# A graph and expert network on one core: down projections loaded from two queues, the last router moved into the first step

## The reference

```python
logits = xf @ gate_w.T                              # 8 experts
topk_w, idx = jax.lax.top_k(logits, 2)
topk_w = jax.nn.softmax(topk_w, axis=-1)
h = jax.nn.silu(jnp.einsum('td,ehd->teh', xf, w1))  # w1: 8 x 1024 x 512
eo = jnp.einsum('teh,edh->ted', h, w2)              # w2: 8 x 512 x 1024
routed = jnp.einsum('te,ted->td', comb, eo)
shared = jax.nn.silu(xf @ sg_gate.T) * (xf @ sg_up.T) @ sg_down.T
x = x + routed + shared
```

## Time and profile before

| | busy us | share | instructions |
|---|---|---|---|
| PE | 589.2 | 95% | 3046 |
| PE's weight loads | 482.8 | 77% | 3046 |
| DVE | 500.8 | 80% | 592 |
| ACT | 430.3 | 69% | 529 |
| POOL | 105.9 | 17% | 112 |

### The profile page before, as it was taken

How to read it: one execution, slowest core, us unless ns; L and a number is a source line. 1 busy time by engine, 2 the same in 40 slices (tenths; PEclk the granted TensorE clock), 3 DMA queues, 4 the chain that set the end, 5 groups by cost and what they waited for, 6 DMA issues and landing times.

```text
span 623.3 us, 9254 instructions
## 1 busy us (share of the span) xinstructions
PE 589.2 (95%) x3046; PEld 482.8 (77%) x3046; DVE 500.8 (80%) x592; ACT 430.3 (69%) x529; POOL 105.9 (17%) x112
## 2 busy tenths in 40 slices
PE   4899999998899999999999999999979989999997
PEld 4677888876688876888888888887768778888886
DVE  6799989884689967898888989898776777777773
ACT  4787787844298859677878787876435766666673
POOL 3100000001000000000000000000011656666666
PEclk9999999999999999999999999999999989999999
DMA  7789999983659966989999999996289989999920
GB/s 252 252 299 307 387 386 385 337 300 107 201 185 343 323 231 235 350 329 341 328 342 355 328 357 331 338 324 221 83 188 215 261 213 266 262 262 262 231 54 17
DMA packets 102224, 168.11 MB, mean 270 GB/s; under 512 B 10683, under 2 KB 30140, under 8 KB 102182
## 3 DMA queue, kind: packets, MB, share of 16 engines
q1 hardware_dynamic: 99876, 165.72, 83.1%
q10 hardware_dynamic: 2322, 2.07, 1.2%
HBM read 167.51 MB, written 0.26 MB: 269 GB/s over the span
## 4 chain that ended last, share of the span: by engine, by line
PE 80%; DVE 11%; ACT 5%; issue 2%; POOL 1%; DMA 1%; SPq 0%; ACTq 0%; DVEq 0%
PE pre L839 31%; PE y L839 31%; PE wt L819 6%; PE tp L851 5%; DVE w_lo L1234 3%; PE pre L846 1%; ACT w_hi L551 1%; DVE w_lo L1221 1%; DVE st L1172 1%; DMA ends<-in_edge_weight 1%; PE y L936 1%; POOL rstd L476 1%; ACT w_hi L538 1%; PE wt L1063 1%; PE pre L952 0%
## 5 line engine op out<-in xcount | busy, mean ns | idle before, releaser
L1234 DVE TENSOR_TENSOR w_lo<-raw,w_hi 128x2048 fp32r<-128x2048 f32 x115 | 259.0, 2287 | 40.0 <-ACT w_hi L551 39.5
L551 ACT ACTIVATE w_hi<-raw 128x2048 fp32r<-128x2048 f32 x116 | 218.6, 1918 | 0.0
L839 PE MATMUL pre<-w_hi,x_hi 128*128 128x512 f32 x292 | 85.1, 404 | 4.0 <-ACT x_hi L556 3.3
L538 ACT ACTIVATE w_hi<-wt 128x512 fp32r<-128x512 f32 x88 | 52.2, 600 | 51.5 <-PE wt L819 50.9
L839 PE MATMUL pre<-w_lo,x_hi 128*128 128x512 f32 x292 | 83.3, 398 | 1.4 <-DVE w_lo L1234 0.9
L606 ACT ACTIVATE hT_hi<-tp 128x512 fp32r<-128x512 f32 x66 | 39.6, 600 | 65.1 <-PE tp L851 65.1
L1221 DVE TENSOR_TENSOR w_lo<-wt,w_hi 128x512 fp32r<-128x512 f32 x88 | 58.5, 668 | 31.2 <-ACT w_hi L538 31.0
L839 PE MATMUL pre<-w_hi,x_lo 128*128 128x512 f32 x292 | 82.9, 397 | 0.0
L839 PE MATMUL y<-w_hi,hT_hi 128*128 128x512 f32 x280 | 81.9, 414 | 0.0
L475 POOL TENSOR_SCALAR rstd<-mv 128x1 f32<-128x1 f32 x11 | 3.0, 272 | 441.1 <-DVE mv L1173 441.1
L839 PE MATMUL y<-w_lo,hT_hi 128*128 128x512 f32 x280 | 75.9, 392 | 0.4 <-DVE w_lo L1234 0.4
(11 more groups left out here) (266 smaller groups left out, 689.6 us busy)
## 6 DMA issues: line engine op xcount, KB each, us to landing
raw<-in_L_ffn_w SPq DMA_DIRECT2D x80, 1024.0 KB, 7.0
raw<-in_L_ffn_W SPq DMA_DIRECT2D x32, 1024.0 KB, 10.2
raw<-in_L_ffn_w SPq DMA_DIRECT2D x32, 512.0 KB, 11.2
raw<-in_L_gnn_Wr SPq DMA_DIRECT2D x8, 1024.0 KB, 6.2
raw<-in_L_gnn_Wl SPq DMA_DIRECT2D x8, 1024.0 KB, 6.6
raw<-in_L_gnn_W SPq DMA_DIRECT2D x2, 1024.0 KB, 7.1
raw<-in_L_ffn_sg_gate SPq DMA_DIRECT2D x2, 1024.0 KB, 8.1
raw<-in_L_ffn_sg_up SPq DMA_DIRECT2D x2, 1024.0 KB, 7.7
```

Of the source, the lines that this page charges most:

```text
L538: act.activation(w_hi[:, g % SPLIT_SLOTS, q], wt[q % 2][:], ACT.Copy).then_inc(w_hi_ready, 1)
L551: act.activation(w_hi[:, g % SPLIT_SLOTS], raw[:, g % RAW_SLOTS], ACT.Copy).then_inc(w_hi_ready, 4)
L839: last = pe.matmul(dst, xs[:, k], ws[:, k], start=start and i == 0, stop=stop and i == len(passes) - 1 and bias is None)
L1234: dve.tensor_tensor(w_lo[:, i], raw[:, g % RAW_SLOTS], w_hi[:, i].bitcast(F32), ALU.subtract).then_inc(w_lo_ready, 4)
```

## The change

1. The four DMAs of a down pair are shared: SP issues q = 0 and 1, at the places where it issued all four; ACT issues q = 2 and 3, with the same waits. ACT does this for pair 0 in the attention layer behind the copy of qT (L773), for pair 2 behind the ReLU for `fT` (L800), and for pair s+2 in the even steps s = 2 to 14 behind the quarters and ahead of SiLU.
2. The router's logits go between the two products of step 0 on PE. DVE reads them out and makes the maximum at the head of step 0, ACT's exponential stands behind the second quarter of step 0, and the rest of `route_l3` stands on DVE behind the quarters of step 1.
3. On ACT, SiLU of step 0 stands behind the quarters, as in all other steps.
4. BRIDGE for the last mixture is 6 instead of 14.

```diff
@@ -27,7 +27,7 @@
 RAW_SLOTS = 8
 SPLIT_SLOTS = 4
 
-BRIDGE = {"l0g": 0, "l0f": 4, "l1f": 37, "l2g": 23, "l2f": 30, "l3g": 28, "l3f": 14}
+BRIDGE = {"l0g": 0, "l0f": 4, "l1f": 37, "l2g": 23, "l2f": 30, "l3g": 28, "l3f": 6}
 SIM_AT = 12
 FIRST_HOTS = 2
 EARLY_COUNTS = 4
@@ -65,7 +65,7 @@
         self.turned = turned
         self.summed = summed
         self.act, self.lead = act, lead
-        self.route = lead or 1
+        self.route = 0 if lead else 1
         self.selected = selected
 
     def chunk(self, s):
@@ -309,6 +309,11 @@
             wv = w.rearrange("e (k c p) n -> e p k c n", c=KC, p=P)
             return wv[at(u // U, 4 // U, it)][:, u % U]
 
+        def pair_rows(slot, q):
+
+            rows = raw[32 * q:32 * q + 32, slot:slot + 2].rearrange("j s c n -> j (s c n)")
+            return rows.rearrange("j (b m) -> j b m", m=2 * P)
+
         def half_rows(w, u):
 
 
@@ -385,9 +390,8 @@
                     wait_split(sp, G_L3G + slot - 1)
                 else:
                     sp.wait_ge(w_blocked, at(4 * (v - 2), 4 * LOOP_BLOCKED, it))
-                for q in range(4):
-                    dst = raw[32 * q:32 * q + 32, slot:slot + 2].rearrange("j s c n -> j (s c n)")
-                    sp.dma_start(dst.rearrange("j (b m) -> j b m", m=2 * P), columns[q]).then_inc(landed[slot], 16)
+                for q in range(2):
+                    sp.dma_start(pair_rows(slot, q), columns[q]).then_inc(landed[slot], 16)
 
             def square(w):
                 return w.rearrange("(c p) n -> p c n", p=P)
@@ -549,6 +553,17 @@
                 else:
                     act.wait_ge(landed[g % RAW_SLOTS], at(arrived(g), 16, it))
                     act.activation(w_hi[:, g % SPLIT_SLOTS], raw[:, g % RAW_SLOTS], ACT.Copy).then_inc(w_hi_ready, 4)
+
+            def load_down(v, it=None):
+
+                slot = raw_slot(BLOCKED[v])
+                columns = both_halves(A["L3_ffn_sg_down"] if v == 0 else A["L3_ffn_w2"][at((v - 2) // 2, 2, it)])
+                if v < 4:
+                    wait_split(act, G_L3G + slot - 1)
+                else:
+                    act.wait_ge(w_blocked, at(4 * (v - 2), 4 * LOOP_BLOCKED, it))
+                for q in (2, 3):
+                    act.dma_start(pair_rows(slot, q), columns[q]).then_inc(landed[slot], 16)
 
             def round_x(tag, plain):
 
@@ -608,8 +623,6 @@
 
                 def shared_step(s, g, it=None):
 
-                    if s == 0:
-                        activate(s)
                     turning = G_L3F + 3 if s == 0 else turned_within(g) if s < pipe.n else None
                     if turning is not None:
                         act.wait_ge(chunk_done, at(turning - SPLIT_SLOTS + 1, 8, it))
@@ -619,15 +632,18 @@
                             round_turned_quarter(turning, q, it)
                         if 0 <= v < pipe.n and s < pipe.n:
                             round_block(BLOCKED[v], q, it)
-                    if 0 < s < pipe.n:
+                        if s == pipe.route and q == 1:
+                            after0()
+                    if s >= 2 and s % 2 == 0 and s + 2 < pipe.n:
+                        load_down(s + 2, it)
+                    if s < pipe.n:
                         activate(s, it)
                     if 1 <= s <= pipe.n:
                         high_turned(s, it)
                     if s == pipe.n - 2:
                         for q in range(4):
                             round_block(BLOCKED[s], q)
-                    if s == pipe.route:
-                        after0()
+
                 for s in range(4):
                     step(s)
                 with act.Fori(0, pipe.loops()) as it:
@@ -771,6 +787,8 @@
             act.activation(h[:, 1], pre[1][:], ACT.Copy).then_inc(sm("l3g_k"), 1)
             act.wait_ge(sm("l3g_qT"), 1)
             act.activation(scratch[:, 2 * D:3 * D], tp[:], ACT.Copy).then_inc(sm("l3g_qTs"), 1)
+            load_down(0)
+
             def turned_pair(g, first):
 
                 if first == 0:
@@ -798,6 +816,7 @@
             turned_pair(G_L3F + 1, 2)
             act.wait_ge(sm("l3g_f1"), 1)
             act.activation(fT[0:32, :], ms[0:32, 0:P], ACT.Relu, bias=l3b1[:, 0:1]).then_inc(sm("l3g_f1s"), 1)
+            load_down(2)
             turned_pair(G_L3F + 2, 0)
             turned_pair(G_L3F + 2, 2)
             round_x("l3f", True)
@@ -887,6 +906,8 @@
                         low = (sm("xlo"), nth("xlo", pipe.tag))
                     if s < pipe.lead:
                         product(g, pre[s % 2][:], x_hi, x_lo, True, True, low=low)
+                        if s == 0:
+                            router()
                         product(g + 1, y[s % 2][:], x_hi, x_lo, True, True)
                     elif s < pipe.n:
                         bias = None
@@ -896,7 +917,7 @@
                                     bias_hl[:, col:col + D])
                         product(g, pre[s % 2][:], x_hi, x_lo, True, True, it, bias, low)
                         g += 1
-                    if s == 0:
+                    if s == 0 and not pipe.lead:
                         router()
                     if s == 3 and seeded:
                         turn_gates(pipe.tag, E8)
@@ -1273,6 +1294,8 @@
                 def step(s, it=None):
                     g = pipe.chunk(s)
                     if pipe.lead:
+                        if s == pipe.route:
+                            router[0]()
                         turning = G_L3F + 3 if s == 0 else turned_within(g) if s < pipe.n else None
                         for q in range(4):
                             if turning is not None:
@@ -1282,8 +1305,8 @@
                     if s < pipe.n:
                         split_chunk(g + AHEAD, it)
                         g += 1
-                    if s == pipe.route == 2:
-                        router()
+                    if s == 1 and pipe.lead:
+                        router[1]()
                     if s == 3 and seeded:
                         copy_gates(pipe.tag)
                     if 1 <= s <= pipe.n:
@@ -1608,16 +1631,18 @@
             split_turned_quarter(G_L3F + 2, 3)
             low_x("l3f")
 
-            def route_l3():
+            def logits_l3():
                 logits_in("l3f", E8)
                 negative_max("l3f", E8)
+
+            def route_l3():
                 dve.wait_ge(sm("exp"), nth("exp", "l3f"))
                 link(top(row[:, 0, 0:E8], E8, 2, row[:, 1, 0:E8], row[:, 2, 0:E8]))
                 link(dve.reduce_sum(row[:, 7, 3:4], row[:, 2, 0:E8], AX_X))
                 link(dve.reciprocal(row[:, 7, 4:5], row[:, 7, 3:4]))
                 link(dve.memset(gates[:, 0:1], 1.0))
                 link(dve.tensor_scalar(gates[:, 1:1 + E8], row[:, 2, 0:E8], row[:, 7, 4:5], None, ALU.mult))
-            pipeline(L3F, route_l3, 1, False)
+            pipeline(L3F, (logits_l3, route_l3), 1, False)
 
 
 _INS = ["x", "src", "dst", "edge_weight", "L0_gnn_emb_1", "L0_gnn_emb_2", "L0_gnn_alpha_p", "L0_gnn_beta_p",
```

## The result

The changed kernel takes 643.97 us (median of 4 runs, 641.47 to 647.17) against 627.42 for the kernel before beside it: a ratio of 1.026 (95% interval 1.022 to 1.030). It is slower by 16.5 us where I had forecast 2.9 us faster. The profiled execution took 643.1 us with a span of 641.4, 18.1 longer than the span before.

A forecast was written before the change was run, and what follows sets the result against it. TensorE, busy 95% of the span near full clock, was taken as the bound. Router -2.77, bridge -0.25 and ScalarE's issues +0.1 gave -2.9 us, taking the 627.52 median to 624.6; range 622.7 to 628.4.

The forecast's parts named there:

- the steady steps: Last dense layer, ten steps of 7.71 us, PE busy throughout at full clock: reordering could win nothing, only lose.
- The router: Moved to steps 0 and 1 of the last layer: losses 1.85 instead of 4.62 us, gain 2.77.
- Step 3: Last layer: its 3.98 us loss, from a 2.14 us wait of PE and lower clock, would go.
- the wait for the later SiLU: PE's third turn of step 1, last layer: wait near 1.0 us, 1.15 lost with a restart; bounds 0.5 to 2.4.
- that in step 2: PE's wait in step 2, last layer: near 0.4 us; step loss 0.7, upper bound 1.5; router taken as 2.2.
- B: Rival, step 0: SiLU's table load waits until ACT is empty, 1.28 us more; 627.6 us in all; chance 0.07.
- E: Rival, step 0: the exponential still takes its own table load, 1.28 us more; 625.5 us in all; chance 0.05.
- The bridge: Ahead of the last layer, BRIDGE 14 to 6: -0.25 us; bounds -0.25 to +1.7 if the clock stays low.
- ScalarE's issues: Half of each down pair issued by ACT, nine pairs: +0.1 us, 0 in steady steps; SyncE's gain worth nothing.
- Rival C: Steady steps: ACT's halves land late, each of seven pairs holds PE 1.0 to 1.1 us; 632 us; chance 0.10.
- The limit: Steady steps: ACT's pieces may take 12.5 us from issue to landing before PE is held.
- The landing: Down-pair pieces land after 7.5, 11.4, 15.6 us (least, median, most); ACT's would be behind none of SyncE's.

The follow-up runs named there:

- e2: Kernel before with the change's router and SiLU places alone, all loads on SyncE, BRIDGE 14: 624.74 us, ratio 0.9961.
- e7: Kernel before with BRIDGE 6 instead of 14 and nothing else: 627.89 us, ratio 1.0024.
- e8: As e2, with 18 filling transposes in PE's wait ahead of the last turned quarter before the layer, and BRIDGE 16: 623.50 us, ratio 0.9955.
- e5: As e1, but ScalarE issues its later pieces at the end of the step before, right behind hT_hi: 626.20 us, ratio 0.9995.
- e12: As e1, but each later up chunk loads only half its rows, 512 KB: 627.56 us, ratio 1.0002.
- e3: The whole change with BRIDGE 14 instead of 6: 635.62 us, ratio 1.010.
- e1: Kernel before with the load split between SyncE and ScalarE alone; router, SiLU and bridge as before: 639.09 us, ratio 1.025.
- e6: The whole change with ScalarE's issue of later pairs moved to the end of the step before: 626.20 us, ratio 0.9991.
- e9: The change with ScalarE's issue at the end of the step before, 18 filling transposes and BRIDGE 16: 624.18 us, ratio 0.9959.
- e10: As e1, with ScalarE's issue behind its wait for the split-weight buffer at the step's head: 627.62 us, ratio 1.0005.
- e11: As e1, with ScalarE's issue behind its fourth rounding of the step: 627.19 us, ratio 0.9999.

## Why the prediction was wrong

**What bounds.** Right: the steady steps could only be lost, and they were.

**The router.** Right. Step 3 takes 7.72 with no wait and at full clock; e2 gives 2.4 us (0.3 to 4.6) for 2.77 forecast. The wait for the later SiLU was put at 1.0 and is 0.92, that in step 2 at 0.4 and is 0.85, since the router took 2.8 us and not 2.2. Rivals B and E fell by ACT's timeline: the exponential without a load, and 1.30 us from the load's start to the SiLU's.

```profile
482.31 0.29 ACT L658 ACTIVATE row<-row 128x8 f32<-128x8 f32 x1
...
484.70 1.28 ACT L616 ACT_TABLE_LOAD   x1
486.00 0.60 ACT L616 ACTIVATE h<-pre 128x512 f32<-128x512 f32 x1
```

The drain that the Trainium skill, "ScalarE: Activation LUTs", "What ACT_TABLE_LOAD costs", adds to the load doesn't show in this row either: the load ends at 485.98, the SiLU starts at 486.00.

**The bridge.** The wrong end of its bounds. I took -0.25 with +1.7 as the other end; alone it measures +1.5 (0.1 to 2.9). The case I named myself (the clock stays low through the first product) is what happened: PE waited 1.81 us for XN where I had said about 1, and in the changed kernel the clock was 0.50 or near it until about 480, longer than the one product. The -0.25 itself came: from the turn of the last quarter to that of XN it is 3.29 us (468.41 to 471.70), before 3.54 (466.98 to 470.52). The lower clock took more. In e7 a part came back in step 3, where the clock didn't fall; after the router's move there is no such fall to save.

**ScalarE's issues.** Right that they cost ScalarE next to nothing: the idle time they leave is 0.16 us ahead of the SiLU at 515.41 and 0.41 ahead of that at 533.58. That SyncE gains nothing by them doesn't hold in every execution: four issues of a pair took it up to 9.04 us in e8, and that held PE; two took it 0.9 in e5.

**Rival C is what happened, and the step that failed is its sizing.** The sum counted nothing for late landings in the steady steps; they cost 15.7 us in the trace. The limit was right: 12.5 us forecast, 12.6 measured. The landing wasn't. I took it from the earlier trace rows, pieces that left SyncE together, and argued that ScalarE's would be quicker, being behind none of SyncE's. They were slower, 11.9 in the median and 21.8 at most, because ScalarE's place puts them beside the next up chunk (issued at 514.27 and at 532.19, ScalarE's at 514.42 and 532.61). e12, with half of that traffic gone, lands them in 9.3 at most. Two rows on record spoke for it: the most in the earlier trace rows, 15.6, was already over the limit, and in the earlier trace rows the DMA share was 1.04 over all ten steady steps. Here the engines had no gap into which a transfer 7 us late could move. A chance of 0.10 wasn't what these rows bore out.

The form of the sum was off as well. I priced 1.0 to 1.1 for each of seven pairs, 7.5; the trace has three waits, of 2.29, 9.31 and 1.01, and 2.7 us of lower clock behind the long one, which the price left out. A pair that lands late also shifts the issues behind it, and the loss comes in lumps. How large depends on details that these runs don't settle: late issue costs 9 us in e3 against e2, 15 in e1, 17 in the change against e6, each by the ratios.

## What to carry to other kernels

When a transfer is moved to another engine's stream, compute first when that engine reaches the issue, then the time to use, and set it against landings in the traffic that will flow at that moment, not in today's. Where the DMA share shows no gap, the landing time isn't a property of the transfer, and its longest row counts, not its median. Place the issue behind the last work that ends before the buffer comes free: one call a few lines higher made 17 us here.

## What the runs showed of the hardware

Two queues with the same bytes, from 516 to 548: issued together from SyncE and ScalarE, the DMA engines have a share of 0.84 for 259 GB/s in e5 (0.91 or 0.92 for 270 to 272 in e6, e9 and e10), from SyncE alone 1.09 for 263 in the kernel before (1.08 or 1.09 for 261 to 264 in e2, e7 and e8). ScalarE's pieces land in 12.7 us at most in e5 and 13.2 in e6, where the four of SyncE needed up to 15.6. One issue of SyncE takes 0.49 us at most in e5, and up to 2.99 in the kernel before and 4.17 in e8. The kernel's time is the same. The Trainium skill, "DMA: Bandwidth & Descriptors", section "Issuing engines are not separate DMA queues", says that several issuing engines only save sequencer time. For the kernel's time the runs agree; in the share and the landings, e5 shows more than that. Why the same engines, without a gap, gave only 210 GB/s when the halves were 5.7 and 8.6 us apart is open.

The clock doesn't answer the same wait in the same way each time: behind the wait of 2.14 us in step 3 it was 0.83 over ten us in the kernel before, and 1.00 in e7, which had run at half the clock from 468 to 476. What decides isn't shown: e11 had run at 0.57 in the same eight us, with BRIDGE 14, and behind the same wait its clock was 0.83.
